# Two decoder layers on one core: the experts' weights split during the first attention and kept in main memory, and another order in the first context stage

## The chip, the cores and the metric

The kernel runs on one core of a Trainium2 chip. The metric is the device time of one execution in microseconds (us); lower is better.

## What is computed

Two decoder layers over x of 16 sequences x 256 tokens x 128 features, with a context of 16 x 64 x 128. Layer 0, in order:

```python
x = x + attention(layernorm(x))      # 16 heads of 64, causal, a slope per head; then @ Wo + bo
x = x + context_gate(layernorm(x), ctx)
x = x + experts(layernorm(x))        # 8 experts of 512, the best 2 per token, and a shared one
```

and in the context gate, which the change concerns:

```python
attn = leaky_relu(einsum('bsd,bqd->bsq', context, query), 0.1)
attn = attn / (norm of attn over q)
a = softmax(swapaxes(attn, 1, 2) * 9, axis=2)     # over the 64 context rows
weighted = einsum('bqs,bsd->bqd', a, context)
cat = concatenate([query, weighted], axis=2)
h = tanh(cat @ W_lin + b_lin);  g = sigmoid(cat @ W_gate + b_gate)
return query * g + h * (1 - g)
```

Layer 1 has the same three parts in other sizes; it is not changed.

## The kernel before

Every engine has its own program, written out by hand; the engines meet at semaphores. Nothing is scheduled by a planner: the order of the code is the order of each engine's queue. Between stages all engines meet at a barrier.

**First attention** (`layer0_attention`). A loop over the 16 batches; a batch has 8 slots p = 0 to 7, one for each pair of heads, and the work on a pair is spread over slots: scores in slot p, normalisation in p + 1, turn of the probabilities in p + 2, product with the values in p + 3. `has_unit(p, lag)` says whether the unit that lies that far back exists. TensorE (`slots`): scores (L315), turns (L361), the projections of q and k of the next slot (L303 to L305, three products of rounded and rest parts: `w_hi`, `w_lo`, `hi`, `lo`), the values (L336 to L338), product (L351); in slot 3 the output projection of the batch before (L371), in slot 6 the turn of the next batch's normalised rows, in slot 7 the turn of the rows of the batch before (L141). In slot 7 it projects for the next batch from `next_hi` and `next_lo` (`project(b + 1, 0)`), so it waits there for `split_next` (L576) on VectorE. VectorE: minima of the scores (`lows`, L501), reciprocals (L511), normalisation of one head of the pair (L515), copies of values and outputs (L546, L525), layer norms. `LayerNorm.apply` (L124) makes the normalised rows; with `keep_rows` it makes each a second time into `g.rows` (L135), which GpSimd adds to x in `add_rows` (L641). ScalarE: exponentials (L441), copies of q and k (L424) and of turned probabilities (L432), rounding. GpSimd: normalisation of the other head (L622), the inverse roots of the layer norms (L118, L121), the copy `cur_lo` (L613), `add_rows`. SyncE issues all loads at the start, first those of this stage, then the rest (L276), and waits for the rest.

**First context stage** (`layer0_context`). 8 units u of 512 tokens (2 batches), in steps s. TensorE: scores of s (L726); for s - 1 the query's part (L743), the sums over the context rows as a product with `same_batch` (L749, 128x256 elements, so the sums stand on all partitions), the context's part (L755); turn of s - 3 (L764), logits of s - 4 (L771). ScalarE: a tenth of the scores, squares, exponentials of s, tanh twice of s - 1, layer norm's `apply` and `keep` of s - 3. VectorE: leaky maximum of s, a reciprocal of the sums (L933) and the product with it (L935) of s - 1, the gate's arithmetic (L941, L948, L952) and statistics of s - 2. GpSimd: roots. SyncE loads the experts' 4 MB of gate and up weights into `in_lo` (L707) and 2 MB of `down` (L708). From step 3 on, ScalarE rounds two of 16 weight pieces of 128x512 a step into `in_hi` (L837) and GpSimd leaves the rest in `in_lo` (L894). The experts' stage, which uses them, begins its products at 711 us.

## Time and profile before

| what | us |
| --- | --- |
| median of 3 runs (1607.4 to 1609.68) | 1607.67 |
| the profiled execution's own time | 1606.57 |
| its span, first to last instruction | 1604.8 |
| first attention, in the profiled execution | 0 to 563 |
| first context stage | 564 to 654 |
| TensorE busy in the span | 1454.2 (91%) |
| VectorE busy | 1086.4 (68%) |
| ScalarE busy | 1021.9 (64%) |
| GpSimd busy | 500.5 (31%) |

Busy time is the sum over instructions; a share is of the span, which holds stages with different limits. In rows of the profile PE is TensorE, DVE is VectorE, ACT is ScalarE, POOL is GpSimd, SP is SyncE; "x8" counts instructions that a row holds, and in square brackets stands how long the engine was idle before and what released it. The granted clock is given as a share of 2.4 GHz: 0.50 is the lower of its two levels, 1.2 GHz.

### The profile page before, as it was taken

The page shows a single profiled execution, that of the slowest core. Times are in us where ns is not written, and L with a number is a line of the kernel's source. Part 1 is how long each engine was busy: PE and PEld are TensorE (multiplying, and loading weights), DVE is VectorE, ACT ScalarE, POOL GpSimd, SP SyncE. Part 2 cuts the span into 40 slices and gives each one's busy share as a digit, 9 for nine tenths or more (in the row PEclk, how much of TensorE's full clock was granted, in tenths as well). Part 3 has the DMA queues.
Part 4 walks back from the last instruction along what each step waited for, and adds up shares of the span by engine and source line. Part 5 has one row for each costly group of instructions (what it writes and reads, how often), then busy time and mean ns, then how long its engine had stood idle before and what let it go on. Part 6 is the DMA issues. An engine that isn't in the chain of part 4 may idle for free. (4 is left out here: it accounts for less than half of the span.)

```text
span 1604.8 us, 39544 instructions
## 1 busy us (share of the span) xinstructions
PE 1454.2 (91%) x11655; PEld 1104.2 (69%) x11703; DVE 1086.4 (68%) x3495; ACT 1021.9 (64%) x2734; POOL 500.5 (31%) x845
## 2 busy tenths in 40 slices
PE   7999999999999877779999969988999886999998
PEld 5777777777777644558888846655665555777697
DVE  6776777777777557656666636787778764774665
ACT  7887777777777536366666646666666663653454
POOL 4332333332333226123333222322323204541133
PEclk9999999999999988779999988999999998998999
DMA  6000000000000041001111110000000000000000
GB/s 214 2 0 0 0 0 0 0 0 0 0 0 0 2 164 33 14 16 44 43 43 45 38 55 14 14 7 13 13 13 11 8 1 1 2 1 1 1 27 26
DMA packets 34077, 34.76 MB, mean 22 GB/s; under 512 B 5600, under 2 KB 29792, under 8 KB 33248
## 3 DMA queue, kind: packets, MB, share of 16 engines
q1 hardware_dynamic: 29664, 25.07, 4.8%
q0 software_dynamic: 4352, 8.92, 2.2%
q8 instruction: 32, 0.52, 0.1%
q14 instruction: 29, 0.24, 0.1%
HBM read 25.07 MB, written 8.91 MB: 21 GB/s over the span
## 5 line engine op out<-in xcount | busy, mean ns | idle before, releaser
L622 POOL TENSOR_SCALAR a_prob<-a_prob,a_inv 128x128 f32<-128x128 f32 (+1 forms) x256 | 126.4, 504 | 346.8 <-DVE a_inv L511 346.8
L441 ACT ACTIVATE a_prob<-a_psS,a_low 128x128 f32<-128x128 f32 (+1 forms) x512 | 208.8, 427 | 1.1 <-DVE a_low L501 1.1
L501 DVE CUSTOM_DVE_ANT_0 a_psS<-a_psS,a_bias 128x128 f32<-128x128 f32 (+1 forms) x512 | 167.4, 388 | 37.7 <-PE a_psS L315 18.3
L1805 ACT ACTIVATE a_probT<-a_psZ 128x512 f32<-128x512 f32 x256 | 138.8, 594 | 75.2 <-PE a_psZ L1591 75.2
L1888 DVE TENSOR_REDUCE a_low<-a_psS 128x4 f32<-128x1024 f32 x128 | 156.2, 1220 | 27.0 <-PE a_psS L1591 25.9
L432 ACT COPY a_probT<-a_psT 128x384 f32<-128x384 f32 x256 | 123.2, 481 | 74.3 <-PE a_psT L361 66.1
L361 PE MATMUL a_psT<-ident,a_prob 128*128 128x128 f32 x768 | 132.7, 282 | 4.5 <-ACT a_probT L432 2.4
L1332 POOL DMA_INDIRECT d_rows<-rows_dram,source x72 | 67.9, 943 | 191.2 <-PE e_psX L1414 143.3
L315 PE MATMUL a_psS<-a_qk 64*128 64x128 f32 (+1 forms) x1024 | 119.9, 353 | 1.1 <-ACT a_qk L424 1.0
L361 PEld LDWEIGHTS a_psT<-ident,a_prob 128*128 128x128 f32 x768 | 84.7, 140 | 45.6 <-issue 34.8
L351 PE MATMUL a_psO<-a_probT,a_v 128*64 128x256 f32 (+1 forms) x1024 | 111.5, 339 | 0.6 <-DVE a_o L525 0.6
L441 ACT ACTIVATION_READ_ACCUMULATOR a_prob<-a_psS,a_low 128x1 f32 x512 | 108.9, 213 | 0.0
L424 ACT COPY a_qk<-a_psA 128x512 f32<-128x512 f32 x128 | 75.1, 586 | 42.8 <-PE a_psA L305 42.6
L351 PEld LDWEIGHTS a_psO<-a_probT,a_v 128*64 128x64 f32 x1024 | 62.2, 136 | 40.5 <-issue 21.3
L315 PEld LDWEIGHTS a_psS<-a_qk 64*128 64x128 f32 x1024 | 67.9, 188 | 23.2 <-issue 16.4
L1472 DVE TENSOR_TENSOR e_hid<-e_act,e_psU 128x512 f32<-128x512 f32 x72 | 49.5, 688 | 50.1 <-ACT e_act L1456 50.1
L1456 ACT ACTIVATE e_act<-e_gate 128x512 f32<-128x512 f32 x72 | 45.3, 630 | 55.6 <-DVE e_gate L1469 55.6
L1434 PEld LDWEIGHTS e_psY<-down,e_hidT 128*128 128x128 f32 x576 | 72.9, 191 | 10.4 <-issue 4.8
L1434 PE MATMUL e_psY<-down,e_hidT 128*128 x576 | 76.2, 275 | 1.5 <-ACT e_hidT L1453 1.5
L1586 PE MATMUL a_psS<-a_qk 32*128 32x256 f32 x512 | 66.0, 334 | 12.1 <-DVE a_low L1888 9.7
L1993 POOL DMA_INDIRECT a_back<-sorted_out,slot x64 | 61.6, 963 | 42.7 <-POOLq L64 25.3
L515 DVE TENSOR_SCALAR a_prob<-a_prob,a_inv 128x128 f32<-128x128 f32 (+1 forms) x256 | 70.3, 317 | 4.5
(375 smaller groups left out, 4160.0 us busy)
## 6 DMA issues: line engine op xcount, KB each, us to landing
sorted_out<-e_y SPq DMA_DIRECT2D x72, 64.0 KB, 1.6
in_lo<-in_gate_up SPq DMA_DIRECT2D x4, 1024.0 KB, 6.9
x<-in_x SPq DMA_DIRECT2D x8, 256.0 KB, 6.1
down<-in_down SPq DMA_DIRECT2D x1, 2048.0 KB, 15.1
rows_dram<-rows SPq DMA_DIRECT2D x8, 256.0 KB, 2.2
out<-x SPq DMA_DIRECT2D x8, 256.0 KB, 2.3
d_rows<-rows_dram,source POOLq DMA_INDIRECT x72, 2.7
a_sel_in<-in_sel SPq DMA_DIRECT2D x1, 1024.0 KB, 4.9
```

The lines of the kernel that those rows point to most:

```text
L315: mm = pe.matmul(psS[:, 2 * (p % 2) + k, lo:hi], qk_sb[rows, p % 2, 0, i * P:(i + 1) * P], qk_sb[rows, p % 2, 1, 0:hi - lo], start=True, s ...
L351: mm = pe.matmul(psO[k * DH0:(k + 1) * DH0, lo:hi], v_sb[:, j, h * DH0:(h + 1) * DH0], pt, start=(j == 0), stop=(j == 1), skip_group_check ...
L361: mm = pe.transpose(psT[:, c * P:(c + 1) * P], prob[:, 2 * (q % 4) + k, c * P:(c + 1) * P], g.ident[:])
L424: nc.scalar.copy(qk_sb[:, p % 2, :, :], psA[:]).then_inc(a_kept, 1)
L432: nc.scalar.copy(probT[:, 2 * (q % 2) + k, :], psT[:, 0:CAUSAL]).then_inc(t_kept, 1)
L441: nc.scalar.activation(prob[:, 2 * (p % 4) + k, lo:hi], psS[:, u, lo:hi], ACT.Exp, bias=low[:, u, i:i + 1], scale=-1.0, accum_out=total[:, ...
L501: nc.vector.tensor_tensor_reduce(psS[:, u, lo:hi], psS[:, u, lo:hi], bias0[:, 2 * p + k, lo:hi], 1.0, LEAST, ALU.add, ALU.min, low[:, u, i ...
L515: nc.vector.tensor_scalar(w, w, inv[:, 2 * (q % 2), i:i + 1], None, ALU.mult).then_inc(norm_done[0], 1)
L622: nc.gpsimd.tensor_scalar(w, w, inv[:, 2 * (q % 2) + 1, i:i + 1], 1.0, ALU.mult, ALU.mult).then_inc(norm_done[1], 1)
L1434: mm = pe.matmul(psY[:, 0:D], hidT[:, c * P:(c + 1) * P], g.down[:, bass.ds(e * FC + c, 1), :], start=(c == 0), stop=(c == FC - 1))
L1805: nc.scalar.activation(probT[:, (p + half + 1) % 2, 2 * half + c, :, :].rearrange("p j s -> p (j s)"), psZ[:, c, :], ACT.Exp, scale=-1.0). ...
L1888: v.tensor_reduce(low[:, p % 2, :, :].rearrange("p i (h r) -> p h i r", h=4)[:, 2 * half:2 * half + 2, :, SHIFT], psS[:].rearrange("p c (i ...
```

## The change

1. In the first attention a piece of the experts' gate and up weights is handled in each batch. SyncE loads piece i into `piece_lo` after the rest of the loads has landed and the stores of piece i - 1 have; ScalarE rounds it into `piece_hi` after the exponentials of slot 3; GpSimd leaves the rest in `piece_lo`, a quarter in each of slots 4 to 7; SyncE stores both in `hi_dram` and `lo_dram`, main memory. The context stage loads the ready halves (4 MB each) instead of raw weights and no longer rounds or splits.
2. `split_next` stands before `lows` in slot 6, not after. The second set of rows is no longer made by VectorE; GpSimd copies it (`copy_rows`).
3. In the context stage the sums are taken with the exponentials as weights and a table of 2 columns (`batch_of`), so that 128x4 sums result; VectorE inverts these, TensorE turns them to 4x128, VectorE copies, TensorE spreads them over the partitions (`spread`, psZ), and VectorE multiplies by that. Exponentials and tanh run one step later than before, `keep` and logits share a buffer psN, and the logits are copied unit by unit.

```diff
@@ LayerNorm.apply and a new method
+            if self.keep_rows:
+                dve.wait_ge(self.rows_kept, START + b)
         for k in range(BT):
...
-            nc.vector.tensor_scalar(self.rows[:, j, k, :], *args).then_inc(self.rows_done, 1)
-            if self.keep_rows:
-                nc.vector.tensor_scalar(g.rows[:, bass.ds(b * BT + k, 1), :], *args).then_inc(self.rows_kept, 1)
...
+    def copy_rows(self, pool, b, seen, j=0):
+
+        pool.wait_ge(self.rows_done, b * BT + BT)
+        pool.sem_inc(seen, 1)
+        self.nc.gpsimd.tensor_copy(self.g.rows[:, bass.ds(b * BT, BT), :], self.rows[:, j, :, :]).then_inc(self.rows_kept, 1)
@@ layer0_attention, sync
             sp.wait_ge(rest_in, 16 * len(rest))
+            for i in range(PIECES):
+                if i:
+                    sp.wait_ge(piece_out, 32 * i)
+                sp.dma_start(piece_lo[:].bitcast(F32), d["gate_up"][:, i, :]).then_inc(piece_in, 16)
+                sp.wait_ge(piece_split, 4 * (i + 1))
+                sp.dma_start(g.hi_dram[:, i, :], piece_hi[:].bitcast(F32)).then_inc(piece_out, 16)
+                sp.dma_start(g.lo_dram[:, i, :], piece_lo[:].bitcast(F32)).then_inc(piece_out, 16)
+            sp.wait_ge(piece_out, 32 * PIECES)
@@ scalar
                         exps(b, p, has_unit)
+                    if new and p == 3:
+                        round_piece(b)
...
+            def round_piece(b):
+                act.wait_ge(piece_in, b * 16 + 16)
+                act.sem_inc(act_seen, 1)
+                nc.scalar.copy(piece_hi[:], piece_lo[:].bitcast(F32)).then_inc(piece_rounded, 1)
@@ vector
+                    if prep and p == 6:
+                        split_next(b + 1)
                     if new:
                         lows(b, p, has_unit)
...
-                    if prep and p == 6:
-                        split_next(b + 1)
@@ gpsimd
+            def split_piece(b, at):
+                pool.wait_ge(piece_rounded, b + 1)
+                pool.sem_inc(pool_seen, 1)
+                nc.gpsimd.tensor_tensor(piece_lo[:, at], piece_lo[:, at].bitcast(F32), piece_hi[:, at].bitcast(F32),
+                                        ALU.subtract).then_inc(piece_split, 1)
...
                     if has_unit(p, 1):
                         norm(b, p)
+                    if new and p >= 4:
+                        split_piece(b, slice((p - 4) * P, (p - 3) * P))
...
+                ln.copy_rows(pool, b, pool_seen)
+                pool.wait_ge(ln.rows_kept, START + b + 1)
@@ layer0_context, sync
-            for i in range(4):
-                n = 2 * E // 4
-                sp.dma_start(g.in_lo[:, i * n:(i + 1) * n, :].bitcast(F32), d["gate_up"][:, i * n:(i + 1) * n, :]).then_inc(weights_in[i], 16)
+            sp.dma_start(batch_of[:], d["batch_of"]).then_inc(batch_in, 16)
+            sp.dma_start(spread[:], d["spread"]).then_inc(spread_in, 16)
+            sp.dma_start(g.in_hi[:].bitcast(F32), g.hi_dram).then_inc(hi_in, 16)
+            sp.dma_start(g.in_lo[:].bitcast(F32), g.lo_dram).then_inc(lo_in, 16)
@@ tensor
-                pe.matmul(psX[:, u % 2, S:2 * S], same_batch[:], e_sb[:, u % 2, :], start=True, stop=True).then_inc(z_done, 1)
+                for k in range(2):
+                    mm = pe.matmul(psZ[:, 2 * k:2 * k + 2], e_sb[:, u % 2, k * P:(k + 1) * P], batch_of[:], start=True, stop=True)
+                mm.then_inc(z_done, 1)
+
+            def turn_sums(u):
+                pe.wait_ge(inv_done, u + 1)
+                pe.transpose(psZ[0:4, P:2 * P], inv_sum[:], g.ident[:]).then_inc(inv_turned, 1)
+
+            def spread_sums(u):
+                pe.wait_ge(inv_kept, u + 1)
...
+                for k in range(2):
+                    mm = pe.matmul(psZ[:, S + k * P:S + (k + 1) * P], spread[:, k, :], inv_rows[:], start=True, stop=True)
+                mm.then_inc(inv_spread, 1)
@@ scalar: the order of a step
-            for s in range(UNITS + 3):
+            for s in range(UNITS + 4):
+                if 1 <= s <= UNITS:
+                    exps(s - 1)
                 if s < UNITS:
                     tenths(s)
+                if s >= 4:
+                    keep(s - 4)
+                if 2 <= s < UNITS + 2:
+                    tanhs(s - 2)
+                if s < UNITS:
                     squares(s)
-                if s >= 3:
+                if s >= 4:
+                    keep_logits(s - 4)
+                if 3 <= s < UNITS + 3:
                     apply(s - 3)
-                if s < UNITS:
-                    exps(s)
-                for i in SPLIT.get(s, ()):
-                    round_weights(i)
-                if 1 <= s <= UNITS:
-                    tanhs(s - 1)
-                if s >= 3:
-                    keep(s - 3)
@@ vector
+            def invert(u):
+                dve.wait_ge(z_done, u + 1)
...
+                v.reciprocal(inv_sum[:], psZ[:, 0:4]).then_inc(inv_done, 1)
+
+            def keep_inverse(u):
+                dve.wait_ge(inv_turned, u + 1)
...
+                v.tensor_copy(inv_rows[:], psZ[0:4, P:2 * P]).then_inc(inv_kept, 1)
...
-                v.reciprocal(inv_sum[:], psX[:, u % 2, S:2 * S]).then_inc(inv_done, 1)
-                dve.wait_ge(inv_done, u + 1)
-                v.tensor_tensor(share[:, u % 2, :], e_sb[:, u % 2, :], inv_sum[:], ALU.mult).then_inc(share_done, 1)
+                v.tensor_tensor(share[:, u % 2, :], e_sb[:, u % 2, :], psZ[:, S:2 * S], ALU.mult).then_inc(share_done, 1)
```

A VectorE step of the context stage is now: leaky maximum of s, `invert` of s - 1, the difference of s - 2, `keep_inverse` of s - 1, the product of s - 2, the shares of s - 1, and the rest as before.

What moved is seen in the queues. In the rows below `a_` names tiles of the attention, `c_` of the context stage; line numbers of the change are those of its own file.

ScalarE, batch 0, from the exponentials of slot 3 to the copies of slot 4, before:

```order
L441 ACTIVATE a_prob,a_total<-a_psS,a_low 128x256
L432 COPY a_probT<-a_psT 128x384 [waits a0_t_done,a0_pv_done]
L424 COPY a_qk<-a_psA 128x512 [waits a0_s_done,a0_a_done]
```

and now:

```order
L461 ACTIVATE a_prob,a_total<-a_psS,a_low 128x256
L494 CAST a_piece_hi<-a_piece_lo 128x512 [waits a0_piece_in]
L452 COPY a_probT<-a_psT 128x384 [waits a0_t_done,a0_pv_done]
L444 COPY a_qk<-a_psA 128x512 [waits a0_s_done,a0_a_done]
```

The cast waits for the load of its piece and stands ahead of all of slot 4.

VectorE, in the loop over batches, from slot 5's end to the first minimum of slot 6, before:

```order
L525 COPY a_o<-a_psO 128x256 [waits a0_pv_done]
L133 TENSOR_SCALAR a_ln_rows<-x,a_ln_moments,a_ln_power 128x128 [waits a0_ln_turned,a0_ln_rstd_done]
L135 REGISTER_ALU
L135 TENSOR_SCALAR rows<-x,a_ln_moments,a_ln_power 128x128
L133 TENSOR_SCALAR a_ln_rows<-x,a_ln_moments,a_ln_power 128x128
...
L135 TENSOR_SCALAR rows<-x,a_ln_moments,a_ln_power 128x128
L498 REGISTER_ALU [waits a0_exp_done]
L501 ISA a_psS,a_low<-a_psS,a_bias 128x128 [waits a0_s_done]
```

and now:

```order
L552 COPY a_o<-a_psO 128x256 [waits a0_pv_done]
L133 TENSOR_SCALAR a_ln_rows<-x,a_ln_moments,a_ln_power 128x128 [waits a0_ln_rows_kept,a0_ln_turned,a0_ln_rstd_done]
L133 TENSOR_SCALAR a_ln_rows<-x,a_ln_moments,a_ln_power 128x128
L603 ISA [waits a0_cur_lo_ready,a0_next_rounded]
L603 TENSOR_TENSOR a_next_lo<-xnT,a_next_hi 128x256
L525 REGISTER_ALU [waits a0_exp_done]
L528 ISA a_psS,a_low<-a_psS,a_bias 128x128 [waits a0_s_done]
```

Two row copies are gone and the split stands ahead of slot 6's minima; before, it followed slot 6's copy of outputs.

TensorE, a full step of the context stage, before:

```order
L726 MATMUL c_psX<-xnT,ctxT 64x256 x2
L743 MATMUL c_psP<-wcat,xnT 128x256 x2
L749 MATMUL c_psX<-c_e,c_same_batch 128x256
L771 MATMUL c_psL<-router,xnT 128x8 x4
L755 MATMUL c_psP<-c_cw,c_share 128x256 x2
L743 MATMUL c_psP<-wcat,xnT 128x256 x2
L755 MATMUL c_psP<-c_cw,c_share 128x256 x2
L764 MATMUL c_psN<-ident,rows 128x128 x4
```

and now:

```order
L765 MATMUL c_psX<-xnT,ctxT 64x256 x2
L791 MATMUL c_psZ<-c_batch_of,c_e 128x2 x2
L782 MATMUL c_psP<-wcat,xnT 128x256 x2
L796 MATMUL c_psZ<-ident,c_inv_sum 4x128
L826 MATMUL c_psN<-router,xnT 128x8 x4
L803 MATMUL c_psZ<-c_inv_rows,c_spread 128x128 x2
L810 MATMUL c_psP<-c_cw,c_share 128x256 x2
L782 MATMUL c_psP<-wcat,xnT 128x256 x2
L810 MATMUL c_psP<-c_cw,c_share 128x256 x2
L819 MATMUL c_psN<-ident,rows 128x128 x4
```

One sum over 256 columns became two over 2 columns, and a turn and two spreading products were added.

## Rows read from the trace of the kernel before

**Rows 1.** waits of TensorE, 40 to 520 us: in total, times, longest
```profile
PE a_psA L303 <- DVE a_next_lo L576: 7.3, 14, 0.5
```

**Rows 2.** timeline of TensorE, slot 7: start us, us, engine line
```profile
306.14 0.93 PE L315 MATMUL a_psS<-a_qk 64*128 64x128 f32 x8
307.01 0.55 PE L361 MATMUL a_psT<-ident,a_prob 128*128 128x128 f32 x3
308.08 0.38 PE L303 MATMUL a_psA<-a_next_hi,a_w_hi 128*128 128x256 f32 x1 [0.53 <-DVE a_next_lo L576]
...
310.47 0.44 PE L141 MATMUL a_psM<-ident,a_ln_rows 128*128 128x128 f32 x2
```

**Rows 3.** timeline of VectorE, around slots 6 and 7
```profile
303.94 0.35 DVE L133 TENSOR_SCALAR a_ln_rows<-x,a_ln_moments,a_ln_power 128x128 f32 x1 [0.92 <-POOL a_ln_power L121]
...
307.53 0.42 DVE L576 TENSOR_TENSOR a_next_lo<-xnT,a_next_hi 128x256 fp32r<-128x256 f32 x1
...
309.76 0.42 DVE L546 COPY a_v<-a_psM 128x256 f32<-128x256 f32 x1
```

**Rows 4.** timeline of TensorE, context stage
```profile
574.47 0.65 PE L726 MATMUL c_psX<-xnT,ctxT 128*64 128x256 f32 x4
...
597.57 0.65 PE L726 MATMUL c_psX<-xnT,ctxT 128*64 128x256 f32 x4
...
599.55 0.95 PE L771 MATMUL c_psL<-router,xnT 128*128 128x8 f32 x8
602.43 0.70 PE L755 MATMUL c_psP<-c_cw,c_share 64*128 64x256 f32 x4 [1.93 <-DVE c_share L935]
...
605.35 0.65 PE L726 MATMUL c_psX<-xnT,ctxT 128*64 128x256 f32 x4
...
623.61 1.12 PE L726 MATMUL c_psX<-xnT,ctxT 128*64 128x256 f32 x4
```

**Rows 5.** lines of VectorE, two stages: busy us, mean ns, idle
```profile
L511 DVE RECIPROCAL a_inv<-a_total 128x4 f32<-128x4 f32 x110 | 18.8, 171 | 0.0
...
L933 DVE RECIPROCAL c_inv_sum<-c_psX 128x256 f32<-128x256 f32 x8 | 14.0, 1749 | 0.3 <-PE c_psX L749 0.3
```

**Rows 6.** timeline of SyncE's queue, the last load at the start
```profile
29.23 0.43 SPq L276 DMA_DIRECT2D shared_out<-in_shared_out  x1
```

**Rows 7.** waits of SyncE's queue, 0 to 60 us
```profile
SPq L197 <- DMA shared_out<-in_shared_out: 1.9, 1, 1.9
```

**Rows 8.** DMA issues, start and page: KB each, us to landing
```profile
gate<-in_gate SPq DMA_DIRECT2D x1, 256.0 KB, 3.2
...
rows_dram<-rows SPq DMA_DIRECT2D x8, 256.0 KB, 2.2
```

**Rows 9.** timeline of ScalarE, batch 0 and a later batch
```profile
27.20 0.48 ACT L432 COPY a_probT<-a_psT 128x384 f32<-128x384 f32 x1
...
296.43 0.48 ACT L432 COPY a_probT<-a_psT 128x384 f32<-128x384 f32 x1 [3.66 <-PE a_psT L361]
```

**Rows 10.** timeline of TensorE, batch 0
```profile
11.82 1.65 PE L315 MATMUL a_psS<-a_qk 64*128 64x128 f32 x8 [0.68 <-ACT a_qk L424]
...
28.02 0.49 PE L361 MATMUL a_psT<-ident,a_prob 128*128 128x128 f32 x3
```

**Rows 11.** windows: length, busy us, granted clock, DMA share, GB/s
```profile
570.00:574.00 4.00, 4.00 (x12) 3.21 (x12) 1.67 (x3) 0.00 (x0) 0.95 (x3) 0.57 1.01 426
610.00:614.00 4.00, 3.79 (x13) 1.99 (x14) 2.07 (x11) 1.53 (x3) 2.29 (x7) 0.62 0.22 66
```

**Rows 12.** timeline of GpSimd, around slots 6 and 7
```profile
307.53 1.00 POOL L641 TENSOR_TENSOR x<-x,rows  x1
```

**Rows 13.** timeline of VectorE, last units of the context stage
```profile
632.01 0.69 DVE L941 TENSOR_TENSOR c_diff<-rows,c_hid 128x512 f32<-128x512 f32 x1 [1.20 <-ACT c_hid L818]
...
640.39 1.76 DVE L941 TENSOR_TENSOR c_diff<-rows,c_hid 128x512 f32<-128x512 f32 x1 [1.81 <-ACT c_hid L818]
642.24 1.59 DVE L948 SCALAR_TENSOR_TENSOR c_part<-c_gate,c_diff 128x512 f32<-128x512 f32 x1
```

More of the change, by code:

```diff
@@ L221, in layer0_attention @@
         resid = ph.sb("resid", [P, BT, D])
+        piece_hi = ph.sb("piece_hi", [P, F0], F32R)
+        piece_lo = ph.sb("piece_lo", [P, F0], F32R)
+        piece_in = ph.sem("piece_in")
+        piece_rounded = ph.sem("piece_rounded")
+        piece_split = ph.sem("piece_split")
+        piece_out = ph.sem("piece_out")
         next_rounded = ph.sem("next_rounded")
@@ L257, in layer0_attention @@
         W_HEAD, W_REST = slice(0, S), slice(S, H * DH0)
+        PIECES = 2 * E
         @block.sync
@@ L660, in layer0_context @@
         psN = ph.ps("psN", [P, 512])
-        psL = ph.ps("psL", [P, 512])
-        same_batch = ph.sb("same_batch", [P, P])
+        psZ = ph.ps("psZ", [P, 512])
+        batch_of = ph.sb("batch_of", [P, 2])
+        spread = ph.sb("spread", [4, 2, P])
         half = ph.sb("half", [P, 1])
@@ L711, in _ @@
                 sp.dma_start(g.rows_dram[cols(u), :].rearrange("(t p) d -> p t d", p=P), g.rows[:, rows(u), :]).then_inc(rows_out, 16)
+            sp.wait_ge(hi_in, 16)
+            sp.wait_ge(lo_in, 16)
             sp.wait_ge(down_in, 16)
@@ L747, in sums @@
                 if u == 0:
-                    pe.wait_ge(same_set, 2)
-                pe.matmul(psX[:, u % 2, S:2 * S], same_batch[:], e_sb[:, u % 2, :], start=True, stop=True).then_inc(z_done, 1)
+                    pe.wait_ge(batch_in, 16)
+                else:
+                    pe.wait_ge(share_done, u)
+                for k in range(2):
[6 more added lines that the diff above has]
+                pe.wait_ge(inv_kept, u + 1)
+                if u == 0:
+                    pe.wait_ge(spread_in, 16)
+                for k in range(2):
+                    mm = pe.matmul(psZ[:, S + k * P:S + (k + 1) * P], spread[:, k, :], inv_rows[:], start=True, stop=True)
+                mm.then_inc(inv_spread, 1)
             def context_part(u, k):
@@ L770, in logits @@
                     t = UB * u + k
-                    mm = pe.matmul(psL[:, t * E:(t + 1) * E], g.xnT[:, t * P:(t + 1) * P], g.router[:], start=True, stop=True)
+                    mm = pe.matmul(psN[:, k * E:(k + 1) * E], g.xnT[:, t * P:(t + 1) * P], g.router[:], start=True, stop=True)
                 mm.then_inc(logits_done, 1)
@@ L779, in _ @@
                 if 1 <= s <= UNITS:
+                    sums(s - 1)
                     query_part(s - 1, 0)
-                    sums(s - 1)
+                    turn_sums(s - 1)
                 if s >= 4:
@@ L890, in rstds @@
                 nc.gpsimd.tensor_tensor(offset[:], minus_mean[:], power[:], ALU.mult).then_inc(offset_done, 1)
-            def split_weights(i):
-                pool.wait_ge(hi_done, i + 1)
-                nc.gpsimd.tensor_tensor(g.in_lo[:, i, :], g.in_lo[:, i, :].bitcast(F32), g.in_hi[:, i, :].bitcast(F32),
-                                        ALU.subtract).then_inc(lo_done, 1)
-            for s in range(UNITS + 3):
+            for s in range(UNITS + 2):
                 if s < UNITS:
                     lengths(s)
-                if 2 <= s < UNITS + 2:
+                if s >= 2:
                     rstds(s - 2)
-                for i in SPLIT.get(s, ()):
-                    split_weights(i)
-            pool.wait_ge(lo_done, PIECES)
         @block.vector
@@ L974, in _ @@
                     keep_cw()
+                if 1 <= s <= UNITS:
+                    invert(s - 1)
+                if s >= 2:
+                    apart(s - 2)
+                if 1 <= s <= UNITS:
+                    keep_inverse(s - 1)
                 if s >= 2:
@@ L2673, in decoder @@
         g.rows_dram = nc.dram_tensor("rows_dram", (T, D), F32, kind="Internal").ap()
+        g.hi_dram = nc.dram_tensor("hi_dram", (P, 2 * E, F0), F32, kind="Internal").ap()
+        g.lo_dram = nc.dram_tensor("lo_dram", (P, 2 * E, F0), F32, kind="Internal").ap()
         g.sorted_out = nc.dram_tensor("sorted_out", (MOE_BLOCKS * P, D), F32, kind="Internal").ap()
@@ L2748, in layout @@
     tok = np.arange(S).reshape(BT, P)
+    batch_of = np.repeat(np.eye(2, dtype=np.float32), L, axis=0)
+    spread = np.zeros((2, 2, 2, P), np.float32)
+    for k in range(2):
+        spread[k, :, k, :] = batch_of.T
     return {
+        "batch_of": batch_of,
+        "spread": spread.reshape(4, 2, P),
         "sel": sel,
```

57 lines of the change are left out of this document (25 added, 32 removed).

## The prediction

> **What bounds the kernel now.** I read the chain of waits first, then the lines by stage, then the timelines of the two stages that the change touches. The chain that ended last lies wholly in the last expert stage, so it tells nothing of this change; what the change is worth must be read stage by stage.
>
> The first attention runs from 0 to 563 us and is bound by TensorE. The only wait of a matmul there that comes once per batch is for `a_next_lo`, 14 times, 0.5 us each [rows 1]. The timeline of slot 7 of one batch shows it: after the turn at 307.01 the next matmul starts at 308.08, and in the other slots that distance is 0.30, so 0.77 us are lost [rows 2]. VectorE is why: the rows of the previous batch are made from 303.94 after an idle 0.92, the scores' minima of slot 6 follow, and only after them the split `a_next_lo` at 307.53; its copy of the values at 309.76 ends slot 7 [rows 3]. The 0.92 is a wait for the second of GpSimd's two small operations, `a_ln_power`.
>
> The first context stage runs from 564 to 654 us. Eight units go through it. TensorE's first matmul of unit 1 is at 574.47, of unit 7 at 623.61, so 49.1 us for 6 units, 8.2 each [rows 4]. In the unit from 597.57 to 605.35 TensorE works 5.85 of 7.78 us and waits 1.93 for the shares, which stand behind a reciprocal of 128x256 elements that takes 1.75 [rows 4, 5]. After unit 7's first matmul the drain follows, some 30 us to the end of the stage.
>
> **The change, part by part.** The sum is made against the profiled execution's own 1606.57 us; the median of the runs is 1607.67, so 1.1 are added at the end.
>
> *1. ScalarE's new wait in the first batch: +7.2 us.* The new rounding of a piece stands in ScalarE's queue after the exponentials of slot 3, in batch 0 too. SyncE issues the load of this piece only after it has waited for all the other loads. Its last load is issued at 29.23, ends its issue at 29.66, and the wait for it is 1.9, so it lands at 31.56 [rows 6, 7]. A 256 KB transfer takes 2.2 us from issue to landing (`rows_dram`) or 3.2 (`gate`, with others under way) [rows 8]; I take 2.6, as the queues are nearly empty, so the piece is there at 34.2. ScalarE is free at 27.20 [rows 9]. It then rounds (0.51, from the 0.61 of this cast in the context stage less its overlap) and takes the copy of the turned block, 0.48, which starts at 34.75 rather than 27.20 and ends at 35.2. TensorE's turn at 28.02 waits for that copy [rows 10]: 35.2 - 28.0 = 7.2. Queued behind ScalarE's wait are its copies of q and k and all exponentials; nothing else of TensorE can go on, since VectorE and GpSimd wait for those. With 2.2 and 3.2 the ends are 6.8 and 7.8. In the other 15 batches ScalarE has 3.66 us idle after slot 3 [rows 9] and the piece has had most of a 33.8 us batch to come, so the 0.6 us cast costs nothing; without that cover it would cost 0.5 x 15 = 7.5.
>
> *2. The clock after that wait: +2.2 us.* At the stage change TensorE was idle from 558.0 to 564.2 but for one turn, and the granted clock was then 0.57 in the stretch 570 to 574 although TensorE worked all of it [rows 11]. So low clock, 1.2 GHz, follows a gap of this kind for some us of dense work. At the low level the scores of a slot take 1.65 for 8 matmuls [rows 10], at the high level 0.93 [rows 2]. A slot of 3.53 becomes about 6.2. Five microseconds at that level lose 5 x (1 - 3.53/6.2) = 2.2. Ends: 0, if the clock holds, and 3.9 for the 9 us that it lasted at the stage change.
>
> *3. Split moved ahead of the minima, one row copy less: -5.0 us.* VectorE drops two copies of rows (0.26 us each in sequence) from the run-up to slot 6 and moves the split (0.33) from after the minima to before them. Against that, GpSimd does a quarter of a piece in slot 5 ahead of the two operations that VectorE waits for: half of a 128x256 subtraction of 1.00 us [rows 12], 0.4 to 0.5. I take 0.4, as VectorE is idle there. Minima of slot 6 then start 0.4 - 0.52 + 0.33 = 0.21 later, those of slot 7 0.21 - 0.33 = 0.12 earlier. The copy of the values therefore ends at 310.06, not 310.18. TensorE without its wait would reach the turn after it at 310.47 - 0.77 = 309.70 and now has to wait for this copy to 310.11. So the gain is 0.36 of the 0.77 a batch: VectorE is late next. 14 batches give 5.0. Ends: 14 x 0.77 = 10.8 if VectorE keeps up, 14 x 0.2 = 2.8 if the piece costs GpSimd 0.55. GpSimd's other new work (three more quarters, a row copy of about 0.4) falls into its idle time; its correction of slot 7 begins some 0.3 late and is wanted 2 us later. The 32 stores and 16 loads of pieces on SyncE have each a batch's time. The end of the attention has one row operation less ahead of the last turn; against it stands GpSimd's copy: 0.
>
> *4. Context stage, unit to unit: -6.8 us.* The reciprocal now takes 128x4 elements, 0.17 instead of 1.75 [rows 5]; added are two matmuls with 2 columns, one turn and two spreading matmuls on TensorE, a copy of 4x128 on VectorE. The nearest row is the logits' 8 issues in 0.95 us [rows 4], 0.12 each. I count 9 or 10 issues, 1.15 us, less 0.43 for the sum over 256 columns that goes: TensorE's work becomes 5.85 + 0.7 = 6.55. The sums now wait for the exponential that stands first in ScalarE's step; ScalarE is far from full and has it ready. The turn's reply is covered by the first query part and the logits; left open is the product with the shares, about 0.55 from the last spreading matmul to the first context part. That is 7.1 a full unit. The first two periods have no turn or logits and take about 8 (clock) and 6: 8 + 6 + 4 x 7.1 = 42.4 against 49.1. **TensorE becomes the bound of this stage.** Ends: -2 (0.2 us for each small issue instead of 0.12) and -9 (the waits vanish as well).
>
> *5. Context stage, the drain: -3.5 us.* Weights are no longer rounded and split here. VectorE's difference in the last unit took 1.76 while GpSimd split weights, 0.69 in another, and the product after it 1.59 [rows 13], 0.9 more than its kind needs: 2.0 saved. The last long reciprocal saves 1.6. One more pipeline step for tanh costs nothing once the exponentials have run out. ScalarE loses two casts a step, which lay beside other work. Rounded: 3.5; ends -1 and -7. The 8 MB of ready weights and 2 MB of `down` now come by SyncE at the stage's start instead of 6 MB; they are wanted at 711 us. Free.
>
> Sum: 7.2 + 2.2 - 5.0 - 6.8 - 3.5 = **-5.9 us**, 1600.7 for such a profiled execution, and **1601.8 us** for the median.
>
> **A rule weighed.** The slow level in this stage is seen where TensorE waited: granted 0.62 from 610 to 614, right after a wait of this kind [rows 11]. My sum lets the denser new order keep the high level but for one stretch. The Trainium skill, "TensorE: Matmul & The Clock Gate", Part 4: PE-mode transpose, says that turns do not count as activity the way matmuls do. By it, turns and perhaps tiny matmuls would leave the clock low though TensorE is full. In this trace the turns and logits of the drain do run at the low level, but there TensorE also waits, so the trace does not decide. If the rule decides, the rival below comes true.
>
> **The rivals.** (a) *Slower: TensorE at 1.2 GHz is the bound of the context stage.* Before, its slow stretches fell partly into waits; now 6.55 of 7.1 us a unit are its own work, and at the low level such work takes 1.7 times as long (1.65 against 0.93 for like rows). If a quarter of the stretch is low, a unit is 7.1 x 1.19 = 8.45, parts 4 and 5 come to about 0, and the total is 7.2 + 2.2 - 5.0 = +4.4: 1612. It decides from about a fifth of the stretch, where the unit reaches the 8.2 of before. For it: the share of issues with few columns grows. Against: the stretches of low clock before followed 2 us waits, which go. Chance 0.16.
> (b) *Nothing measurable.* The wait in batch 0 and its clock cost 11 and the context stage gives only 5 to 6: within 3.2 us. Chance 0.15, 1607.
> (c) *More than forecast.* VectorE keeps up in slot 7 (-10.8 instead of -5.0) or the drain gives its 7 instead of 3.5: 1596 or 1598.3 for the one or the other, 1592.5 for both. Chance 0.12.
> (d) *The change's loads are there in time.* If the piece landed before slot 3 of batch 0, parts 1 and 2 vanish: 1592.4. Against it speaks that SyncE's last load is issued 2 us after ScalarE is ready. Chance 0.05.
> The forecast's own case, -2 to -11, has 0.52; 0.06 of it lies within 0.2%.
>
> **How the numbers follow.** 0.2% is 3.2 us, about what a measurement of this kernel can tell. Faster: 0.46 + 0.12 + 0.05 = 0.63. Same: 0.06 + 0.15 = 0.21. Slower: 0.16. The range reaches down through most of (c), leaving out only both together and (d), and takes in (b) and the better half of (a): 1594 to 1611.
>
> **What the profile would show.** Right: ScalarE idle about 7 us before the cast of `a_piece_lo` at 34 us and a low clock behind it; no wait of `a_psA` for `a_next_lo`, but one of the turn of `a_ln_rows` for `a_v`; a batch of 33.4 instead of 33.8 us; context units of about 7 us with TensorE waiting under 0.7 in each; the stage 10 us shorter; VectorE's 128x512 products at 0.69 throughout. The prediction fails if the granted clock between 580 and 640 is below 0.85, if a new wait of over 1 us per unit appears for the spread reciprocals, or if the cast of the first piece does not wait.

## The result: slower, and where the time went

| | us |
| --- | --- |
| changed kernel, median of 7 runs | 1618.77 (1613.62 to 1625.14) |
| kernel before, median of 7 runs | 1607.34 (1603.97 to 1609.68) |
| ratio, 95% interval | 1.0076 (1.0061 to 1.0091) |
| profiled execution of the changed kernel, its span | 1618.77, 1617.0 (before 1606.57, 1604.8) |

Forecast were 1601.8 us and a range of 1594 to 1611. The time is outside it, above its upper end. Cut at the same instructions of TensorE, the two profiled executions differ by 12.2 us:

| stretch | before | after | difference | forecast |
| --- | --- | --- | --- | --- |
| start to the turn of the next batch's rows in batch 0 | 33.62 | 41.80 | +8.2 | +9.4 (parts 1, 2) |
| from there to the context stage | 530.61 | 532.83 | +2.2 | -5.0 (part 3) |
| context stage: start to unit 1's scores | 10.24 | 10.37 | +0.1 | 0 |
| unit 1's scores to unit 7's | 49.14 | 46.01 | -3.1 | -6.8 (part 4) |
| unit 7's scores to the next stage | 31.26 | 36.23 | +5.0 | -3.5 (part 5) |
| all that follows | 949.93 | 949.76 | -0.2 | 0 |

**Batch 0** is read in three queues. SyncE's timeline (answers to [rows 6]): the last load, then the load of piece 0, after a wait of 1.5.

```profile
28.82 0.43 SPq L288 DMA_DIRECT2D shared_out<-in_shared_out  x1
30.74 0.33 SPq L293 DMA_DIRECT2D a_piece_lo<-in_gate_up  x1
```

ScalarE's timeline and TensorE's ([rows 9], [rows 10]):

```profile
33.51 0.62 ACT L494 CAST a_piece_hi<-a_piece_lo 128x512 fp32r<-128x512 f32 x1 [6.12 <-DMA a_piece_lo<-in_gate_up]
```

```profile
34.66 0.88 PE L381 MATMUL a_psT<-ident,a_prob 128*128 128x128 f32 x3 [6.20 <-ACT a_probT L452]
35.46 1.55 PE L371 MATMUL a_psO<-a_probT,a_v 128*64 128x256 f32 x8
36.94 1.39 PE L335 MATMUL a_psS<-a_qk 64*128 64x128 f32 x8
```

ScalarE stands 6.12 us before the cast, TensorE 6.20 before the turn, and behind it the scores take 1.39 instead of 0.93 [rows 2]: the low clock. The turn comes 6.6 us later than before (28.02), where 7.2 were forecast, and the low clock behind it costs 1.5 instead of 2.2: the mechanism as forecast, 1.2 us smaller.

**A later batch** takes 34.02 us instead of 33.81. VectorE's timeline, slots 5 to 7 ([rows 3]), then GpSimd's over the same time ([rows 12]), then TensorE's ([rows 2]):

```profile
314.04 0.60 DVE L133 TENSOR_SCALAR a_ln_rows<-x,a_ln_moments,a_ln_power 128x128 f32 x2 [1.34 <-POOL a_ln_power L121]
314.56 0.42 DVE L603 TENSOR_TENSOR a_next_lo<-xnT,a_next_hi 128x256 fp32r<-128x256 f32 x1
...
318.88 0.85 DVE L542 TENSOR_SCALAR a_prob<-a_prob,a_inv 128x128 f32<-128x128 f32 x2
319.65 0.40 DVE L575 COPY a_v<-a_psM 128x256 f32<-128x256 f32 x1
```

```profile
312.61 0.45 POOL L646 TENSOR_TENSOR a_piece_lo<-a_piece_lo,a_piece_hi 128x128 fp32r<-128x128 f32 x1
...
317.45 0.46 POOL L646 TENSOR_TENSOR a_piece_lo<-a_piece_lo,a_piece_hi 128x128 fp32r<-128x128 f32 x1
317.85 0.40 POOL L140 COPY rows<-a_ln_rows 128x256 f32 x1
318.50 0.73 POOL L678 TENSOR_TENSOR x<-x,rows  x1 [0.26 <-POOL rows L140]
```

```profile
316.93 0.55 PE L381 MATMUL a_psT<-ident,a_prob 128*128 128x128 f32 x3 [0.18 <-DVE a_prob L542]
...
320.20 0.43 PE L146 MATMUL a_psM<-ident,a_ln_rows 128*128 128x128 f32 x2 [0.53 <-DVE a_v L575]
320.78 0.93 PE L335 MATMUL a_psS<-a_qk 64*128 64x128 f32 x8
```

Three things are to be seen. The rows wait 1.34 for GpSimd, not 0.92: the quarter of slot 5 stands ahead. VectorE's normalisation of slot 7 takes 0.85 and not 0.55, for GpSimd's addition to x runs from 318.50 to 319.23, beside it; a quarter and the copy of rows have pushed it there. And TensorE has exchanged one wait of 0.53 (for `a_next_lo`) for two, 0.18 for `a_prob` and 0.53 for `a_v`. The Trainium skill, "SBUF — State Buffer", "SBUF: two separate sides", says that VectorE and GpSimd share a pair of ports, which for some of VectorE's operations the instruction that started first holds until it ends; the 0.85 agrees with it: 0.55 from the end of the addition at 319.23 gives 319.78, and the normalisation ended at 319.73.

**The context stage**, TensorE's timeline ([rows 4]): scores of units 4 to 7, and one wait and one query part.

```profile
605.02 0.65 PE L765 MATMUL c_psX<-xnT,ctxT 128*64 128x256 f32 x4
...
609.44 0.70 PE L810 MATMUL c_psP<-c_cw,c_share 64*128 64x256 f32 x4 [0.51 <-DVE c_share L987]
...
612.36 0.65 PE L765 MATMUL c_psX<-xnT,ctxT 128*64 128x256 f32 x4
...
620.89 0.98 PE L765 MATMUL c_psX<-xnT,ctxT 128*64 128x256 f32 x4
...
631.01 1.05 PE L765 MATMUL c_psX<-xnT,ctxT 128*64 128x256 f32 x4
...
637.00 2.08 PE L782 MATMUL c_psP<-wcat,xnT 128*128 128x256 f32 x4
```

Windows of 4 us of the same stage ([rows 11] has the columns):

```profile
610.00:614.00 4.00, 4.00 (x25) 2.61 (x24) 1.77 (x11) 1.45 (x3) 1.61 (x5) 1.00 0.22 66
...
618.00:622.00 4.00, 4.00 (x17) 1.85 (x15) 0.73 (x6) 0.19 (x2) 1.57 (x4) 0.57 0.22 66
...
626.00:630.00 4.00, 4.00 (x13) 1.87 (x11) 1.52 (x10) 0.56 (x2) 1.82 (x5) 0.50 0.22 66
```

A unit at high clock takes 7.34 us (605.02 to 612.36), 7.1 were forecast. In the windows from 618 and from 626 TensorE works all of the 4 us at a granted clock of 0.57 and 0.50: the next unit takes 8.53, the one after 10.12. The 0.51 is the only wait that the timeline shows in a unit with logits. Between 580 and 640 the granted clock is 0.84, just under the 0.85 that the prediction had named as a sign of its failure.

**The drain**, ScalarE's timeline:

```profile
652.59 0.78 ACT L890 ACTIVATE xnT<-c_psN,affine 128x512 f32<-128x512 f32 x1 [5.27 <-PE c_psN L819]
653.27 0.59 ACT L875 ACTIVATE c_hid<-c_psP 128x512 f32<-128x512 f32 x1
...
654.51 0.19 ACT L894 COPY logits<-c_psN 128x32 f32<-128x32 f32 x1 [0.17 <-PE c_psN L826]
654.60 1.65 ACT L885 ACTIVATE rows<-x,c_offset,c_power 128x128 f32<-128x128 f32 x4
```

The tanh of the last unit, whose input TensorE had ready by 651.6, stands behind `keep`, which waits for a turn that ends at 652.5. The rows of unit 6 stand behind `keep_logits` of unit 5, though their `c_offset` was there at 650.89.

### The profile page after: what moved, and what is told of

It reads as the page before. It is cut to its first block and busy times, and to the rows that moved or that the text cites. A ratio compares the mean times of both kernels' runs of the same rounds, so it can differ in the third digit from the quotient of the medians.

```text
span 1617.0 us, 39913 instructions
## 1 busy us (share of the span) xinstructions
PE 1468.1 (91%) x11758; PEld 1113.6 (69%) x11759; DVE 1066.3 (66%) x3471; ACT 1026.7 (63%) x2741; POOL 507.5 (31%) x906
## 5 line engine op out<-in xcount | busy, mean ns | idle before, releaser
L444 ACT COPY a_qk<-a_psA 128x512 f32<-128x512 f32 x128 | 75.1, 587 | 33.6 <-PE a_psA L325 33.5
L1490 PEld LDWEIGHTS e_psY<-down,e_hidT 128*128 128x128 f32 x576 | 73.0, 191 | 10.2 <-issue 4.3
L542 DVE TENSOR_SCALAR a_prob<-a_prob,a_inv 128x128 f32<-128x128 f32 (+1 forms) x256 | 74.7, 334 | 4.5
## 6 DMA issues: line engine op xcount, KB each, us to landing
in_hi<-hi_dram SPq DMA_DIRECT2D x1, 4096.0 KB, 12.2
down<-in_down SPq DMA_DIRECT2D x1, 2048.0 KB, 27.4
```

What stands on the lines that cost most here:

```text
L444: nc.scalar.copy(qk_sb[:, p % 2, :, :], psA[:]).then_inc(a_kept, 1)
L542: nc.vector.tensor_scalar(w, w, inv[:, 2 * (q % 2), i:i + 1], None, ALU.mult).then_inc(norm_done[0], 1)
L1490: mm = pe.matmul(psY[:, 0:D], hidT[:, c * P:(c + 1) * P], g.down[:, bass.ds(e * FC + c, 1), :], start=(c == 0), stop=(c == FC - 1))
```

## The experiments

Ratios are to the kernel before, run on the same chip at the same time. In the comparisons of e5 to e8 every kernel, the one before too, took some 23 us longer, in layer 1's attention; they too are read by their ratio. "Stage" is the context stage in the profiled execution, from its first matmul to the next stage's.

### Batch 0: e1

```diff
+            sp.dma_start(piece_lo[:].bitcast(F32), d["gate_up"][:, 0, :]).then_inc(piece_in, 16)
             for dst, src in rest:
```

> Piece 0 is loaded ahead of the loads of the rest, all else as changed. Theory (first batch pays): ScalarE's 6.1 us wait before its first cast and the low clock behind it made batch 0 8.2 us longer than before; both vanish, so the context stage starts at about 566.4 us instead of 574.6 and the whole is 8 us less than the changed kernel (about 1610.5). Rival (the other loads pay): one more 256 KB ahead of them makes loads late that batch 0 needs, and the gain is under 6 us. If the context stage still starts after 572, the loss was not in batch 0.

Ratio 1.0015 (0.9987 to 1.0042), median 1608.68. The cast is at 27.07 without a wait, the context stage begins at 566.48: 8.15 us earlier. The loss of batch 0 was this wait and its clock. The runs lie between 1599.82 and 1619.66, and the stage, not touched, took 82.25 us in this profile instead of 92.61. So something else moves the time by more than most terms of my sum. The drain moved most: 28.57 us in this profile and 36.23 in the changed kernel's, by the same instructions in the same order. The first query part of the last unit shows the clock, in e1 and then in the changed kernel:

```profile
627.77 1.11 PE L783 MATMUL c_psP<-wcat,xnT 128*128 128x256 f32 x4
```

```profile
641.78 2.05 PE L782 MATMUL c_psP<-wcat,xnT 128*128 128x256 f32 x4
```

### The batches: e2, e4, e7

e2, GpSimd:

```diff
-                    if new and p >= 4:
-                        split_piece(b, slice((p - 4) * P, (p - 3) * P))
+                    if new and p == 4:
+                        for k in range(4):
+                            split_piece(b, slice(k * P, (k + 1) * P))
```

> GpSimd leaves all four quarters of a piece in slot 4, where it stands idle over 2 us, none in slots 5 to 7. Theory (GpSimd's queue): the quarter in slot 5 made the rows of the batch before 0.43 us late, and the quarter and copy in slot 6 pushed the addition to x into VectorE's normalisation of slot 7 (0.85 instead of 0.55 us). Without them a batch goes from 34.03 us to about 33.4, the two waits (for a_v 0.53, for a_prob 0.18) go or halve, and the whole is 8 to 9 us less than the changed kernel. Rival (the row copy is what pushes the addition): rows come 0.4 earlier but the normalisation of slot 7 stays at 0.85; a batch of 33.7, 4 us less.

A batch of 33.53 us, the context stage from 567.80: 6.8 earlier. GpSimd's addition, then VectorE's normalisation of slot 7, in e2:

```profile
314.27 0.73 POOL L679 TENSOR_TENSOR x<-x,rows  x1 [0.26 <-POOL rows L140]
```

```profile
315.06 0.55 DVE L542 TENSOR_SCALAR a_prob<-a_prob,a_inv 128x128 f32<-128x128 f32 x2
```

They no longer meet: 0.55. Of TensorE's waits only that for `a_v` is left, 0.24. The rival falls. Ratio 1.0035 (1.0017 to 1.0052).

e4 is the kernel before with `split_next` moved:

> The kernel before, with only the split of the next batch's input moved ahead of slot 6's minima; no pieces, the rows made twice by VectorE, context stage as before. Theory of the prediction (VectorE late next): TensorE's wait for a_next_lo goes, a wait for a_v comes, of the 0.77 us a batch some 0.36 remain as gain: a batch of 33.44 instead of 33.80, 5 us less than before. Rival (nothing gained: the copy of the values stands at the same time, since VectorE does the same work between): a batch of 33.7 to 33.8, less than 1.5 us.

A batch of 33.82, ratio 0.9996 (0.9982 to 1.0011): nothing, as the rival said. TensorE's timeline shows why:

```profile
308.20 0.55 PE L361 MATMUL a_psT<-ident,a_prob 128*128 128x128 f32 x3 [0.28 <-DVE a_prob L515]
...
311.18 0.43 PE L141 MATMUL a_psM<-ident,a_ln_rows 128*128 128x128 f32 x2 [0.24 <-DVE a_v L548]
```

The split ahead of slot 6's minima pushes its normalisation back by 0.33, and slot 7's first turn waits for that. The 0.53 is paid as 0.28 and 0.24.

e7 adds the row copy on GpSimd to e4 (`copy_rows` as in the change), still without pieces:

> The kernel before with the whole of the attention's new order, but no pieces: the split ahead of slot 6's minima, and the second set of rows copied by GpSimd. Context stage as before. Theory (VectorE's work before slot 7 is what counts): 0.52 us less of it, rows not delayed by a piece: a batch of 33.3 to 33.4 instead of 33.81, the context stage from 557 to 558 us, 6 to 7 us less than before. Rival (the row copy on GpSimd pushes its addition to x into VectorE's normalisation, 0.85 instead of 0.55 us): a batch of 33.6, 3 us less.

A batch of 33.53, the context stage from 560.20, 4.0 earlier and not 6 to 7 as the theory said; ratio 0.9990 (0.9976 to 1.0003). That is the batch of e2: with the quarters in slot 4 the pieces cost nothing, spread over slots 4 to 7 they cost 0.5 a batch. The 0.28 gained is the row copies' alone.

### The drain: e3

```diff
-                if s >= 4:
+                if 4 <= s <= UNITS:
                     keep(s - 4)
                 if 2 <= s < UNITS + 2:
                     tanhs(s - 2)
+                if s > UNITS:
+                    keep(s - 4)
...
+                if s >= UNITS:
+                    keep_logits(s - 4)
```

> Only ScalarE's order in the last steps of the context stage differs: tanh ahead of the copy of the turned rows from step 9 on, the rows' application ahead of the copy of the logits from step 8 on. Theory (the drain is a chain through ScalarE's queue): tanh of the last unit starts 1.0 us earlier, the rows of unit 6 no longer stand behind logits; the stage is 2 to 2.5 us shorter (92.6 to about 90.3). Rival (the low clock bounds the drain): TensorE's turns and logits are the long terms of each round (1.11 and 1.88 us), and the stage gets less than 1 us shorter.

The same units as in the changed kernel to 0.01 us (8.53, 10.12), and the drain 33.71 instead of 36.23: 2.5 us. ScalarE's queue cost that much. It is not the largest part: with ScalarE's order as in the changed kernel the drain took 28.57 in e1, 36.33 in e2, 29.07 in e6 and 28.99 in e9 (both below), so the clock alone moves it by 7.7 (e1 against the changed kernel). Ratio 1.0054 (1.0019 to 1.0090).

### Together, and the context stage alone: e5, e8

> The three edits together: piece 0 loaded first, all quarters in slot 4, ScalarE's order in the drain. Theory (three separate costs that add): no wait in batch 0 (8.2 us), a batch of 33.53 instead of 34.03 (14 of them: 7.0), the drain 2.4 shorter: 17.6 us less than the changed kernel, the context stage from about 559.6 us, the whole at 1601 if the context stage has the clock that it mostly had. Rival (the context stage's clock decides more than all three): the stage's own length, 82.3, 92.6 and 99.7 us in three profiles of the same stage, swings the whole by up to 17 us, so the median is anywhere from 1593 to 1608 and scatters by over 10 us.

Ratio 0.9972 (0.9948 to 0.9996): 4.5 us faster than before, 17 less than the changed kernel, with runs 19 us apart (1614.88 to 1633.59). The three costs add: 17.6 were expected, and the context stage begins at 560.08.

e8 has the attention of before, the new context stage, and the weights rounded and split in steps 3 to 10 as before:

> Attention as in the kernel before; the context stage with the new sums and the new order, but the weights loaded raw and rounded and split in steps 3 to 10 by ScalarE and GpSimd, as before. Theory (the new sums and order gain only where the clock is high): a unit at high clock 6.2 to 7.4 us where it was 7.3 to 7.8, but a stage of 88 to 95 us because low stretches and the longer drain take it back; the median within 4 us of before with a scatter over 8 us. Rival (the pieces' work in the attention is the whole loss, the context stage gains its 8 to 10 us): a stage of 82 us and a median of 1598 to 1600.

Ratio 1.0022 (1.0006 to 1.0039), a stage of 97.28 us at a clock of 0.71. The new stage by itself loses some 3.5 us (by the interval 1.0 to 6.4); its units at high clock take 7.4.

### The clock: e6, e9, e10, e12

e6, the changed kernel plus:

```diff
                     spread_sums(s - 1)
+                    for k in range(2):
+                        pe.matmul(psX[:, s % 2, S:2 * S], g.xnT[:, 0:P], g.wcat[:, 0, :], start=True, stop=True)
                     context_part(s - 1, 0)
```

> The changed kernel with two more matmuls of 128x256 (into the unused half of the scores' bank, read by nobody) in each of TensorE's 0.51 us waits for the shares, 8 times. Theory A (the clock falls because TensorE does too little in this stage): the granted clock stays high in the units, every unit takes 6.2 to 7.4 us, the stage is 82 to 85 us in every run, the scatter of the times falls from 12 us to a few, and the median is 5 to 8 us lower than that of the changed kernel. Rival B (the clock falls whatever TensorE is given): low stretches as before, each unit 0.1 to 0.2 us longer, the same median and scatter or 1 to 2 us worse.

More work, less time: ratio 1.0035 (1.0021 to 1.0049), some 6.6 us less than the changed kernel, and runs 5 us apart instead of 11.5. The context stage as one window, of the kernel before, the changed one, e1, e2 (all three with the same context stage) and e6; after the colon of each its length, then busy times of PE, PEld, DVE, ACT, POOL, then the granted clock:

```profile
564.23:654.87 90.64, 65.40 (x296) 43.46 (x297) 54.14 (x124) 47.01 (x107) 44.61 (x77) 0.80 0.25 93
```

```profile
574.63:667.24 92.61, 77.26 (x353) 51.99 (x353) 38.01 (x132) 38.76 (x98) 24.61 (x58) 0.74 0.35 137
```

```profile
566.48:648.73 82.25, 66.84 (x352) 45.95 (x353) 37.93 (x132) 38.79 (x98) 24.67 (x58) 0.85 0.40 154
```

```profile
567.80:667.54 99.74, 84.37 (x352) 55.61 (x353) 38.13 (x132) 38.78 (x98) 23.05 (x58) 0.67 0.33 127
```

```profile
574.75:659.36 84.61, 73.30 (x385) 50.40 (x385) 37.92 (x132) 38.78 (x98) 24.68 (x58) 0.88 0.38 150
```

DVE, ACT and POOL do the same work in the three executions of the same stage (within 1.6 us); only TensorE's time and clock differ, by 17.5 us. In e6 the clock stays at 1.00 through units 2 to 7, each 6.7 to 7.8 us; only the stage's start, unit 1 and the last turns and logits are low. Two matmuls (1.13 us) are more than the 0.51 of the wait: each unit pays 0.48 for them.

> The changed kernel with seven PE-mode turns of 128x128 in each wait for the shares, in place of the two matmuls of 128x256 of the run before; both fill about 1.13 us. Theory A (turns do not hold the clock as matmuls do): low stretches from the fifth unit on as in the changed kernel, a stage of 92 to 100 us and no gain over it. Theory B (any work in the wait holds the clock, it is the gap that matters): a stage of 84 to 86 us, the high clock throughout the units, as with the two matmuls (84.6 us).

The seven turns took 0.99. Ratio 1.0022 (1.0012 to 1.0031), stage 85.04 at 0.86, runs 5.4 us apart. This is theory B, but for one later unit with a low stretch (9.25): the turns held the clock nearly as well as the matmuls did. The Trainium skill, "TensorE: Matmul & The Clock Gate", Part 4: PE-mode transpose, against which I weighed my sum, says that turns do not count; for these turns in fp32 the measurement decides against it. The Trainium skill, the same page, "A second HAM failure mode: psum-queue depth-cycling", tells of short idle times between groups of matmuls that bring the clock down again and again; this agrees with a unit that waits 0.37 and 0.51, or only 0.51, and with what filling it does.

> The changed kernel with one matmul of 128x256 (0.57 us) in each wait for the shares, which is 0.51 us long. Theory A (how dense the matmuls of a unit are sets the clock, and one is enough): the clock stays high, units of 6.3 to 7.4 us, 0.4 shorter than with two; the stage 81 to 82 us. Rival B (one is too little): low stretches return in some units, and the runs scatter over 6 us as those of the changed kernel do.

Units of 6.2 to 7.4 but for one with a low stretch (8.97); stage 85.14 at 0.82, ratio 1.0023 (1.0013 to 1.0033), runs 5.7 apart. As good as two, not better: a unit with logits takes 7.39 instead of 7.82, and low stretches in one unit and in the drain (31.84 instead of 29.07) cost that again. One matmul makes such a unit only 0.05 longer than the 7.34 without it, so the gain hardly comes from another timing of the queues.

e12 is the kernel before with three such matmuls ahead of `context_part(s - 1, 0)`:

> The kernel before, its context stage with three filling matmuls of 128x256 (some 1.6 us) in each of the waits of 1.9 to 2.6 us for the shares; nothing else. Theory (the clock of this stage was open to gain before the change too): no low stretches between unit 1 and the drain, units of 7.2 to 7.8 us, the stage 84 to 86 us instead of 90.6, 5 us less than before. Rival (the waits in this order are too long and the reciprocal sets the pace anyway): the stage within 2 us of 90.6.

Stage 85.36 at 0.88, no low clock between unit 1 and the drain, ratio 0.9966 (0.9953 to 0.9980): 5.5 us faster than before by work that computes nothing. The kernel before had lost to the clock too.

### Sums or steps, units or ends: e13 to e16

e13 puts ScalarE's steps back (exponentials of s, tanh of s - 1, `keep` of s - 3) and keeps the new sums:

> The changed kernel with its new sums, but ScalarE's steps as before: exponentials of the same step, tanh one step behind, the turned rows copied in the step of their turn. Theory A (the later steps cost the drain): from unit 7's scores to the next stage 31 us as before instead of 36.2; if the low clock comes from how TensorE's gaps lie, units of 7 to 8 us with a low stretch here and there: a stage of 86 to 90 us, 3 to 6 us less than the changed kernel. Theory B (the small matmuls of the new sums bring the low clock): granted clock of the stage 0.67 to 0.76 as in the changed kernel, low in most of units 4 to 7, and a stage above 90.

Stage 83.69 at 0.85, drain 28.96, ratio 1.0056 (1.0035 to 1.0078), runs from 1609.57 to 1625.19. The drain is 7.3 us shorter than the changed kernel's, as theory A says, but the run doesn't show theory A: e1, with the new steps, had a drain of 28.57 when the clock was high as long as here. By these two profiles the new steps cost the drain nothing where the clock is high. The median is 3 us below the changed kernel's, with intervals that overlap, and the scatter stays. The 0.85 does not decide on theory B either, as e1's profile had it too.

e14 has `same_batch` and the long reciprocal back in the new steps:

> The changed kernel with its new steps, but the sums as before: one product with a table of 128 columns and a reciprocal of 128x256 that takes 1.75 us. Theory A (the later steps cost the drain): 35 to 37 us from unit 7's scores to the next stage. Theory B (the small matmuls bring the low clock): the granted clock at 0.80 or more, as before the change. Both expect units near 7.8 us, since the wait for the shares behind the long reciprocal is back: a stage of 94 to 97 us and 2 to 4 us more than the changed kernel under A alone, 90 to 92 under B.

Neither: ratio 1.0158 (1.0142 to 1.0173), units of 9.2 to 10.5 after a first of 6.8, stage 102.05. VectorE's reciprocal of 1.75 now stands behind the gate's arithmetic, which waits for tanh, and TensorE waits 3.0 for the shares. So the run loses 25 us against the kernel before; of its profile's 22.1, 9.3 stand ahead of the stage, as in the changed kernel, and 11.4 in it. The new steps do not go with the old sums, and the run says nothing of the clock.

> The three repairs with one filling matmul in each unit's wait for the shares and none at the ends. Theory (the clock of the units is most of the gain): a stage of 80 to 83 us, 0.993 to 0.995 of the kernel before, scatter of some 5 us. Rival (the ends are most of it): 0.996 to 0.997, as with the repairs alone.

Ratio 0.9898 (0.9881 to 0.9916), median 1591.11, runs 4 us apart, stage 83.02. Better than expected.

> The three repairs with filling matmuls only at the stage's ends (behind the last output projection, around the barrier, in the drain) and none in the units. Theory (the clock of the units is most of the gain): first part 6.4 us instead of 9.8, drain of about 26, but low stretches in the units: a stage of 80 to 90 us, 0.992 to 0.996, scatter over 8 us. Rival (the ends are most of it, a clock that is high at the start stays): a stage of 75 to 77 us and 0.989 to 0.991.

The first part is 6.40, as expected, and the low stretches in the units come all the same: units up to 10.2, stage 92.21 at 0.75. Ratio 0.9941 (0.9925 to 0.9958). A high clock at the start doesn't stay.

e11 has both fillings:

> The three repairs (first piece loaded first, quarters in slot 4, ScalarE's order in the drain) with filling matmuls: one in each wait for the shares, one before each turn and each logits of the last steps, seven after the last output projection of the attention, one after its last turn, two before the first scores. Theory (costs of clock and queue are separate and add): context stage from 560 us; its first 10 us at high clock, 4 to 5 us shorter; the units 6.2 to 7.4; the drain 26 to 28 instead of 33.7: a stage of 76 to 80 us, and the whole 0.987 to 0.991 of the kernel before, with a scatter of some 4 us. Rival (the clock stays low behind the barrier whatever is filled): the first 10 us as before, a stage of 83 to 86 us and 0.992 to 0.995.

```profile
559.85:635.53 75.68, 68.42 (x382) 45.75 (x383) 37.91 (x132) 38.47 (x98) 24.84 (x58) 0.97 0.43 167
```

Ratio 0.9897 (0.9881 to 0.9914), median 1591.43 against 1606.86. It and e15 beat both kernels. The stage is 7.3 us shorter than in e15, but what follows it took 954.4 us against 948.4, and the medians are the same. One profile of each does not tell whether the ends' gain is given back or lost to chance.

## Why the prediction was wrong

**Parts 1 and 2 (+9.4, measured +8.2): right.** The mechanism, its place and its clock are as written; the piece landed at 33.5, not 34.2, because SyncE issued its last load 0.4 earlier and waited 1.5, not 1.9. e1 takes it all away.

**Part 3 (-5.0, measured +2.2): wrong in two steps.** "VectorE is late next" was followed only along the copy of the values. The sentence "Minima of slot 6 then start 0.4 - 0.52 + 0.33 = 0.21 later" had a consequence that I left out: slot 7's first turn had 0.06 of room (306.95 to 307.01) and waits for slot 6's normalisation. e4 shows it alone: no gain. The second is "GpSimd's other new work falls into its idle time". GpSimd was idle, but its addition came 1.3 us later, beside VectorE's normalisation, which then took 0.30 longer; e2 shows it by taking it away. The 0.4 for the quarter in slot 5 was right (0.43). The row copies, costed as part of the same 0.52, are the whole gain: 0.28 a batch (e7).

**Part 4 (-6.8, measured -3.1): mechanism right at the high clock, undone by the low one.** The first four periods, all at high clock but for a low stretch in the old kernel's first, went from 30.88 to 27.36; the last two, both with low stretches, from 18.26 to 18.65. e1, with a low stretch mainly in the fifth, took 43.57 for the six, against 42.4 forecast and 46.01 here. "My sum lets the denser new order keep the high level but for one stretch" is the step that failed. Denser did not mean a higher clock: 0.74 in the stage after 0.80. Rival (a), at 0.16, had this effect: it put parts 4 and 5 at about 0, and they came to +1.8; its 1612 was too low because it took over part 3. Of its argument, that turns and issues with few columns leave the clock low, the turns' half is refuted by e9; matmuls of few columns were not tried by themselves.

**Part 5 (-3.5, measured +5.0): the same step failed.** The sum had no term for the clock in the drain; it too rests on the high level of the sentence above. From 635.84 to the turn at 651.52 every product of the changed kernel ran at the low level (2.05 to 2.08 for a query part), where the kernel before had run the same two query parts in 1.13 and 1.03 (629.57, 631.76). Nearly all of the 8.5 us between forecast and time is this: with a high clock there the same code took 28.57 (e1), 7.7 less than here and 2.7 less than before. At the low clock a second step failed. "One more pipeline step for tanh costs nothing once the exponentials have run out" looked at the tanh's input and not at ScalarE's queue, in which `keep` and `keep_logits` stood ahead of work that was ready; that cost 2.5 us at the low clock (e3), and the forecast had no term for it. What it costs at the high clock was not measured. VectorE's products at 0.69 were right.

**The loads** of 10 MB in the context stage landed 12.2, 23.0 and 27.4 us after their issue and cost nothing, as forecast. Not shown is why low stretches begin where they do: three executions of the same stage had 82.3, 92.6 and 99.7 us.

## What to carry to other kernels

Where a change makes an instruction earlier or later by a few tenths of a us, follow every reader of it in the next slot, not the one wait that is to go; and give work to an idle engine only where it pushes nothing of its queue beside an instruction that it slows. Before a stage is made denser, look at its granted clock: this one had 5.5 us (e12) to 12 us (e15 after e5) to gain from a few matmuls in its waits that compute nothing, as much as the whole change was to bring or twice that. One profile of such a stage is not enough to read a loss from: here the drain alone took 28.6 or 36.2 us by the same code. In a pipeline's last steps, write the order of each queue by what is ready, not by the loop's.

## What the runs showed of the hardware

- In the changed kernel TensorE worked 4.00 of 4.00 us in each of two windows at a granted clock of 0.57 and 0.50 (618 to 622, 626 to 630), in a stage in which it waits 0.51 of 7.34 us a unit; with this wait filled the clock was 1.00 for over 50 us on end (e6, 592 to 648).
- With seven PE-mode turns of 128x128 (0.99 us) in the wait the stage took 85.04 us at 0.86, with two matmuls of 128x256 (1.13 us) 84.61 at 0.88.
- The same stage, with the same work on the other engines, took between 82.3 and 99.7 us, its drain between 28.6 and 36.3.
- VectorE's normalisation in SBUF took 0.85 instead of 0.55 us beside GpSimd's addition of 128x256.
